# Turns and norm transposes one step further behind their producers, and a rotation made of one VectorE product and two GpSimd adds

## What is computed

```python
mod = (silu(c) @ wmod).reshape(4, 6, 1, -1)      # sa, ca, ga, sb, cb, gb
h = layernorm(x) * (1 + ca) + sa
q, k, v = split(h @ W_qkv.T)                     # 16 heads of 32
q, k = rope(q), rope(k)                          # x * cos + rotated(x) * sin
p = softmax(causal(q @ k.T / sqrt(32)))
x = x + ga * ((p @ v) @ W_o.T)
h = layernorm(x) * (1 + cb) + sb
x = x + gb * moe(h)                              # 16 experts, the best two of each token
```

## Time and profile before

| | us |
|---|---|
| median of 3 runs | 1788.76 (1788.75 to 1792.32) |
| profiled execution | 1794.68 |
| its span, first to last instruction | 1792.9 |

### The profile page before, as it was taken

The page is one execution under the profiler, slowest core; times in us unless marked ns, Lnnn a source line. Parts: engine busy times, 40 slices in busy tenths (PEclk is TensorE's granted clock), DMA queues, the critical chain, the costliest instruction groups (busy, mean ns, idle before and its releaser), DMA issues. The chain is left out here.

```text
span 1792.9 us, 29315 instructions
## 1 busy us (share of the span) xinstructions
PE 1513.2 (84%) x9300; PEld 1060.5 (59%) x9300; DVE 1330.9 (74%) x2591; ACT 736.6 (41%) x1191; POOL 711.3 (40%) x708
## 2 busy tenths in 40 slices
PE   5379999899999879999988999999856899999700
PEld 0256665556566556656655565665425799999600
DVE  5377778877777987677797767777648677777698
ACT  1024455433445434344543334546410566666400
POOL 3122444443435434333543423355414433333275
PEclk9699999989999988999998999999975899999955
DMA  7654334524244443423445342423237344444499
GB/s 273 210 157 147 117 93 140 147 91 159 86 130 126 114 158 96 155 84 123 136 121 156 100 146 84 128 85 95 77 145 315 119 145 146 146 142 146 138 363 341
DMA packets 133473, 263.55 MB, mean 147 GB/s; under 512 B 15960, under 2 KB 69720, under 8 KB 132336
## 3 DMA queue, kind: packets, MB, share of 16 engines
q1 hardware_dynamic: 112368, 189.76, 33.1%
q0 software_dynamic: 11808, 40.90, 7.1%
q10 hardware_dynamic: 9184, 31.46, 4.4%
HBM read 176.03 MB, written 86.03 MB: 146 GB/s over the span
## 5 line engine op out<-in xcount | busy, mean ns | idle before, releaser
L767 DVE TENSOR_REDUCE neg_max<-ring 128x1 f32<-128x512 f32 (+3 forms) x768 | 405.3, 550 | 49.6 <-PE ring L537 34.0
L664 ACT ACTIVATE probs<-ring 128x1024 f32<-128x1024 f32 (+3 forms) x384 | 310.8, 811 | 235.0 <-PE ring L567 173.4
L532 PE MATMUL ring<-stack_t 96*128 96x512 f32 (+3 forms) x768 | 301.7, 415 | 10.8 <-DVE parts L834 10.8
L993 POOL TENSOR_TENSOR rope_a<-rope_a,rope_b 128x256 f32<-128x256 f32 x128 | 127.4, 995 | 395.4 <-DVE rope_b L853 395.4
L509 PE MATMUL ring<-w_parts,h_hi 128*128 128x384 f32 x1024 | 278.2, 353 | 1.6 <-DVE h_lo L827 1.5
L562 PE MATMUL ring<-stack_t 128*128 128x512 f32 (+3 forms) x768 | 253.2, 397 | 7.9 <-ACT probs L664 3.6
L978 POOL TENSOR_TENSOR prob_sum<-prob_sum,probs 128x1024 f32<-128x1024 f32 (+3 forms) x128 | 232.7, 1818 | 25.7 <-ACT probs L664 24.5
L532 PEld LDWEIGHTS ring<-stack_t 96*128 96x128 f32 x768 | 147.7, 197 | 157.6 <-issue 66.6
L509 PEld LDWEIGHTS ring<-w_parts,h_hi 128*128 128x128 f32 x1024 | 184.7, 196 | 2.6 <-DVE h_lo L827 2.5
L509 PE MATMUL ring<-w_parts,h_lo 128*128 128x384 f32 x512 | 174.8, 341 | 0.0
L583 PE MATMUL y_ps<-probs,v_tok 128*32 128x512 f32 (+3 forms) x1536 | 170.0, 516 | 2.3 <-ACT probs L664 2.3
(11 more groups left out here) (155 smaller groups left out, 2488.2 us busy)
## 6 DMA issues: line engine op xcount, KB each, us to landing
stack_t<-stack_dram SPq DMA_DIRECT2D x384, 128.0 KB, 3.0
stack_dram<-parts SPq DMA_DIRECT2D x64, 512.0 KB, 2.7
w_parts<-w_dram SPq DMA_DIRECT2D x32, 768.0 KB, 7.0
y_dram<-y_sb SPq DMA_DIRECT2D x80, 256.0 KB, 2.0
x_in<-x SPq DMA_DIRECT2D x32, 256.0 KB, 3.4
x<-x SPq DMA_DIRECT2D x32, 256.0 KB, 3.3
x_dram<-x SPq DMA_DIRECT2D x32, 256.0 KB, 2.9
h_dram<-h SPq DMA_DIRECT2D x32, 256.0 KB, 2.0
```

What stands on the lines that cost most here:

```text
L532: mm = nc.tensor.matmul(ring[:, BANK[use], 0:width], stack_t[0:MROW, i % 2, 0, h, qt * P:qt * P + P], stack_t[0:MROW, i % 2, 1, h, kc * 51 ...
L664: nc.scalar.activation(probs[:, step % PROBS, :, q0:QC], ring[:, bank:bank + 2, q0:QC], ACT.Exp)\
L767: nc.vector.tensor_reduce(neg_max[:, which, t, h:h + 1], ring[:, BANK[use], 0:width], AX.X, ALU.max, negate=True).then_inc(s_max, 1)
L993: nc.gpsimd.tensor_tensor(rope_a[:, t % 2, :], rope_a[:, t % 2, :], rope_b[:, :], ALU.add)\
```

## The change

All offsets are in steps. PROJECT starts one step earlier; TURN is three steps behind it instead of two; NORM_A is five ahead of it instead of four, NORM_B one behind NORM_A as before, NORM_C three behind NORM_A instead of two; MAX_TURN is two behind MAX_COMBINE instead of one. Whatever is placed relative to these moves with them.

The rotation's three VectorE products become one, of q and k with the cosines and with the sines at once, into a tile of two planes. The halves of a head are no longer exchanged on VectorE but when GpSimd adds, in two instructions. VectorE no longer waits for the previous sum. The softmax's scale moves from the tables into the exponential.

```diff
 def project_step(i, t):
-    return STEPS * (i - 1) + 3 * t - 13
+    return STEPS * (i - 1) + 3 * t - 14

 def norm_step(b, t):
-    return project_step(G * b, t) - 4
+    return project_step(G * b, t) - 5

-TURN = {step + 2: it for step, it in PROJECT.items()}
+TURN = {step + 3: it for step, it in PROJECT.items()}
-NORM_C = {step + 2: bt for step, bt in NORM_A.items()}
+NORM_C = {step + 3: bt for step, bt in NORM_A.items()}
-MAX_TURN = {step + 1: ih for step, ih in MAX_COMBINE.items()}
+MAX_TURN = {step + 2: ih for step, ih in MAX_COMBINE.items()}
...
-                            pe.wait_ge(rope_terms, 3 * (u + 1))
+                            pe.wait_ge(rope_terms, u + 1)
...
-                        pe.wait_ge(roped, NT * i + t + 1)
+                        pe.wait_ge(roped, 2 * (NT * i + t + 1))
...
-                        nc.scalar.activation(probs[:, step % PROBS, :, q0:QC], ring[:, bank:bank + 2, q0:QC], ACT.Exp)\
+                        nc.scalar.activation(probs[:, step % PROBS, :, q0:QC], ring[:, bank:bank + 2, q0:QC], ACT.Exp, scale=SCALE)\
...
-                        if u:
-                            dve.wait_ge(roped, u)
-                        qk = ring[:, BANK[use], 0:256].rearrange("p (s h d) -> p s h d", s=2, d=DH)
-                        nc.vector.tensor_tensor(rope_a[:, t % 2, :].rearrange("p (s h d) -> p s h d", s=2, d=DH), qk,
-                                                trig[:, 0, :, t, :].unsqueeze(2).to_broadcast([P, 2, HG, DH]),
+                        qk = ring[:, BANK[use], 0:256].rearrange("p (h d) -> p h d", d=DH)
+                        nc.vector.tensor_tensor(rope_ab[:, t % 2, :, :].rearrange("p k (h d) -> p k h d", d=DH),
+                                                qk.unsqueeze(1).to_broadcast([P, 2, 2 * HG, DH]),
+                                                trig[:, :, t, :].unsqueeze(2).to_broadcast([P, 2, 2 * HG, DH]),
                                                 ALU.mult).then_inc(rope_terms, 1)
-                        for half in range(2):
-                            lo, src = 16 * half, 16 * (1 - half)
-                            nc.vector.tensor_tensor(
-                                rope_b[:, :].rearrange("p (s h d) -> p s h d", s=2, d=DH)[:, :, :, lo:lo + 16],
-                                qk[:, :, :, src:src + 16],
-                                trig[:, 1, :, t, lo:lo + 16].unsqueeze(2).to_broadcast([P, 2, HG, 16]),
-                                ALU.mult).then_inc(rope_terms, 1)
...
-                        pool.wait_ge(rope_terms, 3 * (u + 1))
-                        nc.gpsimd.tensor_tensor(rope_a[:, t % 2, :], rope_a[:, t % 2, :], rope_b[:, :], ALU.add)\
-                            .then_inc(roped, 1)
+                        pool.wait_ge(rope_terms, u + 1)
+                        a, b = (rope_ab[:, t % 2, k, :].rearrange("p (h two d) -> p h two d", two=2, d=DH // 2) for k in range(2))
+                        for half in range(2):
+                            nc.gpsimd.tensor_tensor(a[:, :, half, :], a[:, :, half, :], b[:, :, 1 - half, :], ALU.add)\
+                                .then_inc(roped, 1)
```

More of the change, by code:

```diff
@@ L187, in adaln_block @@
             w_gate = sb("w_gate", [P, C, E])
-            trig = sb("trig", [P, 2, 2, NT, DH])
+            trig = sb("trig", [P, 2, NT, DH])
             masks_b = sb("masks_b", [P, 2, P], bf16)
@@ L198, in adaln_block @@
             h2_t = sb("h2_t", [P, C, P])
-            rope_a = sb("rope_a", [P, 2, 2 * P])
-            rope_b = sb("rope_b", [P, 2 * P])
+            rope_ab = sb("rope_ab", [P, 2, 2, 2 * P])
             stats = sb("stats", [P, 2, 6])
@@ L227, in adaln_block @@
             mod_sign, mod_size = prob_sum[0:B, 0, 0, :], h2_t[0:B, :, :].rearrange("p c n -> p (c n)")
-            masks_f = rope_a[:, 0, :].rearrange("p (k n) -> p k n", k=2)
+            masks_f = rope_ab[:, 0, 0, :].rearrange("p (k n) -> p k n", k=2)
             const_in = sem("const_in")
@@ L240, in _ @@
                     for k, (dst, src) in enumerate([(ident_f[:, :], ident), (masks_f[:, :, :], masks),
-                                                    (trig[:, :, :, :, :], rope), (k_ones_sb[:, :], k_ones),
+                                                    (trig[:, :, :, :], rope), (k_ones_sb[:, :], k_ones),
                                                     (w_out[:, :, :], w_o_t), (w_gate[:, :, :], wg_t),
@@ L518, in turn @@
                             mm = nc.tensor.transpose(ring[:, BANK[use], s * P:s * P + P],
-                                                     rope_a[:, t % 2, s * P:s * P + P], ident_f[:, :])
+                                                     rope_ab[:, t % 2, 0, s * P:s * P + P], ident_f[:, :])
                         mm.then_inc(turn_ps, 1)
@@ L1435, in _constants @@
     cos, sin = np.cos(angle), np.sin(angle)
-    rope = np.stack([np.concatenate([cos, cos], 1), np.concatenate([-sin, sin], 1)])
-    rope = rope.astype(np.float32).reshape(2, 1, NT, P, DH) * np.array([SCALE, 1.0], np.float32).reshape(1, 2, 1, 1, 1)
-    rope = np.ascontiguousarray(rope.transpose(3, 0, 1, 2, 4))
+    rope = np.stack([np.concatenate([cos, cos], 1), np.concatenate([sin, -sin], 1)])
+    rope = np.ascontiguousarray(rope.astype(np.float32).reshape(2, NT, P, DH).transpose(2, 0, 1, 3))
     k_ones = np.zeros((P, HG), np.float32)
```

## The result

| | before | after |
|---|---|---|
| median of 13 runs each | 1788.75 us | 1802.28 us |
| lowest to highest | 1785.91 to 1792.45 | 1795.69 to 1812.51 |
| profiled execution | 1794.68 | 1802.06 (span 1800.3) |

A forecast was written before the change was run, and what follows sets the result against it. TensorE was taken to bound plain groups, VectorE the norm stretches, with a lower clock behind them. Terms -12 -2 -3 -6 -2 -4 +2 +3 gave -24 us: 1770.7 profiled, 1764.8 median, range 1751 to 1790.

The forecast's parts named there:

- Plain groups and turns: TensorE's turn waits for the rotation in the loop: gone with one step more, gain 12 us (6 to 20).
- Norm transposes: Loop waits of 26.1 us: mostly worth nothing, but one a batch gains 2 us each, 6 in all.
- The clock: TensorE at 1.2 GHz behind each batch's last norm tile (0.52 over 14 us): expected to fall there again.
- Order of the banks: Seven banks dealt anew, some columns now following the previous step's exponential: +3 us (0 to 6) for unseen couplings.
- Max turns: Waits of 4.1 us in three places, their results used five steps later: gain 3 us.
- Rotation and sum: Norm tiles: one shorter VectorE product gains 2 us; GpSimd's longer adds colliding with VectorE cost 2 (0 to 8).
- Ahead of the loop: Before the loop: half of 5 idle us and an earlier eighth x tile, together 4 us gained (0 to 7).
- The stall: Wait for the eighth x tile behind each batch's norms: still 6.5 us, change nothing, plus or minus 3 each time.
- rival (d): Behind each batch's norms: x as slow behind the mod rows, stall 10.6 us, 27 us lost, 1792; chance 0.17.
- Rival (b): In the loop: turn waits given back at the next bank, as VectorE's maxima keep their order, 1782; chance 0.18.

The follow-up runs named there:

- e16: Kernel before with the new rotation on the old steps and the second modulation's rows loaded at step 34: 1759.54 us, ratio 0.9824 to the kernel before.
- e17: New rotation, second modulation's rows loaded at step 34, projections one step earlier, turns three behind, norms moved along: 1764.94 us, ratio 0.9859 to the kernel before.
- e11: New rotation, old steps, second modulation's rows a group earlier, first-group weights four steps later, turns alone one step later: 1785.46 us, ratio 0.9965 to the kernel before.
- e18: Changed kernel with the second modulation's rows loaded at step 34: 1784.14 us, ratio 0.9965 to the kernel before.
- e4: Kernel before (old rotation) with statistics and normalisation one step earlier, norm transposes, projections and turns unmoved: 1800.64 us, ratio 1.0041 to the kernel before.
- e14: New rotation, projections one step earlier, turns three behind, second modulation's rows a group earlier, its transposes and logits a step later: 1776.92 us, ratio 0.9908 to kernel before.
- e8: Changed kernel with the rotation's product and adds one step behind the projection: 1989.50 us, ratio 1.1094 to the kernel before.
- e1: Kernel before with the new rotation on the old steps: 1783.39 us, ratio 0.9940 to the kernel before.
- e2: Kernel before with the new steps and the old rotation: 1811.82 us, ratio 1.0102 to the kernel before.
- e5: New rotation, old steps, second modulation's rows a group earlier, weights of a batch's first group four steps later: 1769.83 us, ratio 0.9890 to the kernel before.
- e13: New rotation, second modulation's rows a group earlier, projections one step earlier, turns three behind, norms moved along: 1780.07 us, ratio 0.9911 to the kernel before.

## Why the prediction was wrong

**Plain groups and turns: the size right, the reason only in part.** -12 was forecast for the turns' waits; they went, and the plain groups gained 8.0 us (8.4 from e16 to e17). But by e11 the distance of the turn alone, which also ends these waits, is worth only 3.4 of it. The rest came with the earlier projection, to which the prediction gave nothing.

**Norm transposes: the step that failed.** It booked the removed waits at -6, and of the normalisation that moved two steps it said nothing, since VectorE had the same work to do. But where that work stands in VectorE's queue has a price. e18 against e17 shows it: 21 us in the norms, of which 9.8 are longer work of VectorE, 7.5 of them in the two products of the normalisation, and 11.3 longer idleness, with the lower clock in it. e4, with the normalisation one step earlier and the banks as before, has the same sign: 18 us in the steps 57 to 75. How the 21 us divide between the new places of NORM_B and of NORM_C and the maxima was not separated in e18. The rows to see the idleness were there: VectorE busy for 47.5 of 49.3 us meant that it hardly ever stood at a rotation there, and the question that was not asked is which work kept it from that.

**The clock: a missing term.** The prediction counted it only behind the stall. There its time did not grow (norms: 58.0 us before, 54.6 after), but in "second" it went from 6.8 to 27.3, 9 us, behind waits of 1.5 to 2.5 us of the transposes (L614), whose distance no one changed. They came with the turns and projections (e16 to e17: 0 to 20.5). The turns alone hardly bring them: in e11 TensorE does not wait at L614 in the steps 93 to 99, waits 1.2 to 1.3 us at step 111, and has 3.4 us at the lower clock in "second". Of the kernels whose rotation and transposes were not moved, each with the earlier projection has the waits, and each with the old projection and turns has none. So it is the projection's step, alone or with the turn's. e14 reduced them, by moving the transposes.

**Order of the banks: mis-sized.** +3 was taken for new couplings. The three rows of waits for VectorE at L508 and L561 in the kernel after add up to 37.3 us, many of them where VectorE is the limit, and 9.5 of them are those of the norms' new place (L508 for y_t). So what the order of the banks itself cost stays open. e8 shows how steep the ground is: one bank one step longer, 10% (1.109 against 1.008).

**Max turns: -3 forecast.** The waits went. But the last stretch, which has neither norms nor second modulation, takes 42.6 us in each kernel with all new steps and 39.6 in e17. Whether that is the maxima's distance or the deal of banks it brings was not separated; e11, with the maxima where they were and another deal, took 43.7, which speaks for the deal.

**Rotation and sum: -2 and +2 forecast, -10.8 measured (e1).** The durations were right within 0.2 us. What was missing is again the clock, for most of it. The +2 for collisions between VectorE and GpSimd was booked at the wrong cause: the longer pair of adds brought under 1 us (62.6 us for the two products of the normalisation in the norms of e1, 61.9 before), the new place of the norms 8 (70.6 us in the kernel after and in e2).

**Ahead of the loop: -4 forecast.** Up to step 3 it is 2.1 us less.

**The stall: nothing forecast.** The working held: behind the third batch's norms x was issued at T+7.5, wanted at T+10.7 and there at T+15.2, where T+8.1, T+10 and T+16.5 were forecast. So the stall fell from 16.2 to 11.9 us in three places, below the 5 to 8 each that were forecast, and the half clock directly behind it got shorter. So rival (d), the only slower one, had the sign right and the mechanism wrong: the tile did not come later. Rival (b) was nearest in kind, with score columns waiting for maxima (17.9 us), but as priced it could not make the kernel slower.

**VectorE beside GpSimd.** The two kinds of product in the kernel after, with min/median/max in ns:

```profile
L845 DVE TENSOR_TENSOR rope_ab<-ring,trig x128: 675/692/693, 77.8 to 1220.5; 128x512 f32<-128x512 f32 x128
```

```profile
L817 DVE SCALAR_TENSOR_TENSOR x_hat<-x_hat,rstd,mod_b x32: 750/753/2702, 67.5 to 980.3; 128x512 f32<-128x512 f32 x32
```

The rotation reads PSUM and is never held (675 to 693 ns); the normalisation reads SBUF twice and takes up to 3.6 times its least. This agrees with the Trainium skill (SBUF — State Buffer, the section on its two separate sides): there a VectorE operation and a GpSimd one exclude each other only if the former is in a two-port mode or has two SBUF inputs.

## What to carry to other kernels

Before a long instruction of an in-order engine is moved, ask what waits it covers for the instruction behind it, which buffer is freed behind it, and what it will run beside: the cover goes, and its own work can take longer (here 8 us in 24 tiles). Where a few buffers are dealt in a ring, an early release is worth more than a smoother start: with 7 banks, one more step for one use cost 10% here. When parts of a schedule are compared, first clear the transfers that come late, since their stalls and the clock behind them hide differences of the size looked for; in this kernel that clearing (a load moved to an empty place in the queue) was itself worth twice what the rotation gained.

## What was not expected of the hardware

An idle time of 1.53 us of TensorE at the same instruction was followed by 10.2 us at the lower clock, by 3.4 us, and by none. Across kernels with the same instructions the time of the loop at the lower clock went from 14 (e5) to 82 us (after) in norms and "second", and e8, with 143 us of waits for the projection's bank in the rows above, had 201. So a short wait that a sum prices at its own length can cost more again: 4.7 us beside 1.53 in the third batch, nothing in the second. A store of the parts, 2.7 us at the median, took 9 us in e13 behind a group's weights, rows of the modulation and an x tile.
